# A sandwich layer on eight cores: the next block's K projection ahead of the receptance matmuls, or all projections at the block's start

## What is computed

```python
x = x + layernorm(attn(layernorm(x)))   # q,k,v projections, rope, 16 heads of 64,
                                        # band: a query sees itself and the 512 keys before it; wo
x = x + layernorm(ffn(layernorm(x)))

# ffn, per token, x_prev = the token before:
xr = mu_r * x + (1 - mu_r) * x_prev
xk = mu_k * x + (1 - mu_k) * x_prev
r = sigmoid(xr @ W_r.T)
k_act = square(relu(xk @ W_k.T))
out = r * (k_act @ W_v.T)
```

## Time and profile before

| | us |
|---|---|
| median of 2 runs | 6092.82 (6066.61 to 6119.03) |
| the profiled execution | 6056.06 |
| its span on the slowest core (5) | 6054.5 |
| spans of the eight cores | 6033.4 to 6054.5 |
| blocks | 16 |

### The profile page before, as it was taken

One profiled execution on the slowest core, in us unless ns is written; L12 is line 12 of the kernel. 1 busy time (PEld: TensorE's weight loads), 2 busy tenths in 40 slices (PEclk: granted clock), 3 DMA queues, 4 the chain that ended last, 5 costly groups with the idle time before them and its releaser, 6 DMA issues.

```text
span 6054.5 us, 52395 instructions; the slowest of 8 cores (6033.4 to 6054.5 us)
## 1 busy us (share of the span) xinstructions
PE 3191.1 (53%) x11840; PEld 1236.7 (20%) x11840; DVE 2472.7 (41%) x3561; ACT 2120.2 (35%) x3905; POOL 1200.6 (20%) x1028
## 2 busy tenths in 40 slices
PE   0344726557362664737646373673636457364573
PEld 0111212222120221212222121221212122121221
DVE  2353443434344343443435344343443534334342
ACT  0141523415233251533524244161432415244152
POOL 0021212212121121211211122121221212122122
PEclk9957567575675857658576665856658575675757
DMA  6512122120322202122121311303112130311301
GB/s 187 154 42 73 39 80 73 42 84 28 84 70 69 84 29 73 53 70 84 34 74 50 93 56 55 99 8 90 56 59 94 42 91 21 84 70 42 111 1 63
DMA packets 269844, 410.36 MB, mean 68 GB/s; under 512 B 151778, under 2 KB 151778, under 8 KB 269540
## 3 DMA queue, kind: packets, MB, share of 16 engines
q1 hardware_dynamic: 203492, 197.28, 12.3%
q0 software_dynamic: 33792, 134.22, 6.9%
q10 hardware_dynamic: 32256, 75.51, 3.2%
HBM read 297.89 MB, written 75.50 MB: 62 GB/s over the span
## 4 chain that ended last, share of the span: by engine, by line
PE 30%; ACT 20%; DVE 19%; DMA 8%; issue 8%; POOL 7%; SPq 5%; ACTq 2%; DVEq 1%; POOLq 0%
PE pb L521 7%; ACT pk L495 6%; SPq L174 4%; PE pb L488 4%; PE pb L326 4%; DVE ybuf L533 4%; PE pb L678 4%; PE pb L408 3%; PE pb L580 3%; ACT krot L250 3%; ACT krot L253 3%; DVE ax L637 3%; POOL ybuf L755 2%; POOL pk L713 2%; POOL pk L506 2%
## 5 line engine op out<-in xcount | busy, mean ns | idle before, releaser
L533 DVE RECIPROCAL ybuf<-pb 1x512 bf16<-1x512 f32 x256 | 858.0, 3352 | 805.8 <-PE pb L521 797.3
L326 PE MATMUL pb<-vext,Wwk 128*128 128x512 bf16 x1024 | 260.4, 416 | 1666.3 <-DMA vext<-hstage 1624.2
L495 ACT ACTIVATE pk<-pb,neg 128x512 bf16<-128x512 f32 (+3 forms) x1792 | 945.3, 527 | 282.7 <-PE pb L488 26.2
L488 PE MATMUL pb<-qx,krot 64*128 64x512 bf16 (+3 forms) x1792 | 681.0, 434 | 395.1 <-ACT pk L495 308.6
L521 PE MATMUL pb<-pk,vext 128*65 128x128 bf16 (+3 forms) x2368 | 522.9, 404 | 79.2 <-DVE ax L546 33.0
L326 PEld LDWEIGHTS pb<-vext,Wwk 128*128 128x128 bf16 x1024 | 104.4, 105 | 1818.8 <-issue 1727.6
L510 POOL TENSOR_TENSOR pk<-pk,tri4s 128x512 bf16<-128x512 bf16 x256 | 294.2, 1149 | 751.7 <-ACT pk L495 751.7
L506 POOL TENSOR_TENSOR pk<-pk,tri0s 128x512 bf16<-128x512 bf16 x192 | 220.8, 1150 | 1043.8 <-ACT pk L495 1043.8
L326 PE MATMUL pb<-vext,Wwq 128*128 128x512 bf16 x1024 | 256.3, 411 | 248.9 <-DVE scr L350 248.9
L730 PE MATMUL pb<-WS,pk 128*128 128x512 bf16 x1024 | 284.0, 443 | 159.2 <-DVE pk L741 71.4
L488 PEld LDWEIGHTS pb<-qx,krot 64*128 64x128 bf16 x1792 | 165.8, 107 | 965.3 <-issue 965.3
(11 more groups left out here) (105 smaller groups left out, 4046.4 us busy)
## 6 DMA issues: line engine op xcount, KB each, us to landing
xsl<-x SPq DMA_DIRECT2D x128, 512.0 KB, 4.1
WS<-wo_bf POOLq DMA_DIRECT2D x16, 2048.0 KB, 12.4
WS<-wr_bf POOLq DMA_DIRECT2D x16, 2048.0 KB, 21.1
cosb<-cosd SPq DMA_DIRECT2D x128, 256.0 KB, 4.4
sinb<-sind SPq DMA_DIRECT2D x128, 256.0 KB, 4.8
WS<-wk_bf POOLq DMA_DIRECT2D x16, 2048.0 KB, 10.4
WS<-wv_bf POOLq DMA_DIRECT2D x16, 2048.0 KB, 10.1
out<-ybuf ACTq DMA_DIRECT2D x64, 512.0 KB, 2.7
```

Source lines behind the costliest of these rows:

```text
L326: ins = e.matmul(pb[bk][:, :], wsb[:, D * ci + 128 * dc:D * ci + 128 * (dc + 1)], hv[:, BS * ci:BS * (ci + 1)], start=(ci == 0), stop=(ci ...
L488: qlo=qlo, qhi=qhi: e.matmul(pb[bk][:, qlo:qhi], ksrc[po:po + 64, BS * md + 128 * tc:BS * md + 128 * (tc + 1)], qx[po:po + 64, BS * md + q ...
L495: texp = cop("scalar", lambda e, bk=bk, c=c, qlo=qlo, qhi=qhi, pku=pku: e.activation(out=pku[:, BS * c + qlo:BS * c + qhi], in_=pb[bk][:, ...
L533: t_rc = cop("vector", lambda e, rb=recipb[uslot], ub=ub: e.reciprocal(rb, pb[ub][64:65, :]), waits=[t_av, buf.get(("recip", uslot)), prev ...
```

## The change

The blocks are no longer interleaved in that way.

- `planB1` and `planB2` are gone. At the start of each block stand all projections: Q pair 0 (banks 0, 1), K pair 0 (4, 5), Q pair 1 (2, 3), K pair 1 (6, 7), and again with p = 2 and 3; each is followed in DVE's list by its rotation. Cos and sin of a p are loaded once and serve q and k.
- v goes through banks 0 and 1 in turn; each evacuation waits only for its own group and the memset, which stands at the block's start.
- The next block's `planA` stands behind the receptance matmuls and sigmoids and before the keys. It reads the transposed layernorm output into hfm, not into vext.
- Keys use banks 4 and 5, wv2 banks 6 and 7 (both had 2 and 3).
- The square of the relu moves from GpSimd to DVE.
- The scratch tile of the statistics is now always the older vext tile. The debug output, off in both, is removed. Some tokens that guard buffers are other ones.

```diff
-        t_hr = [dmat("sync", "hfm", hv[:, BS * c:BS * (c + 1)], hstage[:, 128 * c:128 * (c + 1)],
-                     waits=[t_hw[-1], av_tok]) for c in range(8)]
+        t_hr = [dmat("sync", "hfm", hfm[:, BS * c:BS * (c + 1)], hstage[:, 128 * c:128 * (c + 1)],
+                     waits=[t_hw[-1], buf.get("hfm")]) for c in range(8)]
...
+        lnsink[0] = vext[1 - par][:, 0:2048].bitcast(F32)
+        onesap = bass.AP(vext[par][:, :].tensor, 64, [[4160, 128], [65, 64]])
+        ones_restore = cop("vector", lambda e, a=onesap: e.memset(a, 1.0),
+                           waits=[kv_cons[par]], tok=True)
...
+        load_cos(0, n)
+        load_cos(1, n)
         for p in range(4):
-            mm = _proj_mms(W["wk"], t_wres["wk"], p, (4, 5) if p % 2 == 0 else (6, 7),
-                           hv, t_hr, extra=[sinkA_tok] if p == 0 else ())
+            q_toks += proj_pair(W["wq"], t_wres["wq"], qx, buf.get("qx"), bqs, p,
+                                (0, 1) if p % 2 == 0 else (2, 3))
+            k_toks += proj_pair(W["wk"], t_wres["wk"], krot[par], kv_cons[par], bks, p,
+                                (4, 5) if p % 2 == 0 else (6, 7))
             if p + 2 <= 3:
-                load_cos(p + 2)
+                load_cos(p + 2, n)
...
-                bk = tj * 2 + hh
+                bk = (tj * 2 + hh) % 2
...
+                tev = cop("scalar", lambda e, oap=oap, bk=bk: e.copy(oap, pb[bk][:, :]),
+                          waits=[tmm, ones_restore], tok=True)
...
-        if it + 1 < niter:
-            pendingA = planA(it + 1, t_av_last)
-
-        if it + 1 < niter:
-            pendingB = planB1(it + 1, pendingA, buf.get("lnstat"))
 
         wr_users = []
         t_rsg = []
...
+        if it + 1 < niter:
+            pendingA = planA(it + 1)
+
         t_wv2 = stream_weight("wv2", 1, wr_users)
...
-            bk = 2 + dk % 2
+            bk = 4 + dk % 2
...
-            tka = cop("gpsimd", lambda e, dk=dk: e.tensor_mul(
+            tka = cop("vector", lambda e, dk=dk: e.tensor_mul(
                 pk2[0][:, BS * dk:BS * (dk + 1)], relu_t[:, :], relu_t[:, :]),
...
-                bk = 2 + hh
+                bk = 6 + hh
```

More of the change, by code:

```diff
@@ L276, in build_core @@
     prev_z = None
+    kv_cons = [None, None]
     kv_tok = [{}, {}]
@@ new lines, in planA @@
+        return t_ln, t_hw, [t_hr[-1]] * 8
+    pendingA = None
+    ones_restore = None
+    for it in range(niter):
+        s, n = it // NB, it % NB
+        par = n % 2
+        rows0 = s * S + n * BS
+        lnsink[0] = vext[1 - par][:, 0:2048].bitcast(F32)
+        onesap = bass.AP(vext[par][:, :].tensor, 64, [[4160, 128], [65, 64]])
+        ones_restore = cop("vector", lambda e, a=onesap: e.memset(a, 1.0),
+                           waits=[kv_cons[par]], tok=True)
+        if it == 0:
+            t_wo = stream_weight("wo", 0, [])
+            t_wr = stream_weight("wr", 1, [])
+            t_ln, t_hw, t_hr = planA(0)
+        else:
+            t_wo, t_wr = next_wo, next_wr
+            t_ln, t_hw, t_hr = pendingA
@@ L309, in _mk_cos, with load_cos @@
         t_cos = {}
[L311 removed]
+        def load_cos(p, n):
             slp = p % 2
[L313 removed]
+            tc1 = dma("sync", "cos%d" % slp, cosb[slp][:, :], cos_d[p, :, n * BS:(n + 1) * BS],
                       waits=[buf.get(("cos", slp))])
[L315 removed]
+            tc2 = dma("sync", "sin%d" % slp, sinb[slp][:, :], sin_d[p, :, n * BS:(n + 1) * BS],
@@ L316, in load_cos @@
                       waits=[buf.get(("cos", slp))])
             t_cos[p] = (tc1, tc2)
[L318 to L350, removed]
-            scr[:, BS:2 * BS], pb[bhi][:, :], bias_sb[:, p + 4:p + 5], cosb[slp][:, :],
-            ALU.add, ALU.mult), tok=True)
-        t6 = cop("vector", lambda e: e.tensor_add(
-            dst[:, BS * (p + 4):BS * (p + 5)], scr[:, 0:BS], scr[:, BS:2 * BS]), tok=True)
-        bank_free[blo] = t5
-        bank_free[bhi] = t5
-        buf["scr"] = t6
-        buf[("cos", slp)] = t6
-        return [t3, t6]
@@ L561, in build_core @@
                 plan_norm(head_order[i - 2])
-        t_dbg = None
-        if dbg and it == 0:
-            t_dbg = dma("sync", "z", dattn[:, :], ax[:, :], waits=t_attn_evac)
+        kv_cons[0] = kv_cons[1] = t_av_last
         wo_users = []
@@ L618, in build_core @@
         t_h2r = [dmat("sync", "hfm", hfm[:, BS * c:BS * (c + 1)], h2stage[:, 128 * c:128 * (c + 1)],
-                      waits=[t_h2w[-1], buf.get("hfm")]) for c in range(8)]
+                      waits=[t_h2w[-1]] + q_toks + k_toks + v_toks + t_sc_all) for c in range(8)]
         t_h2r = [t_h2r[-1]] * 8
```

155 lines of the change are left out of this document (64 added, 91 removed).

## The result

| | before | after |
|---|---|---|
| median, us (lowest to highest) | 6079.07 (6054.11 to 6127.35, 10 runs) | 5725.11 (5718.11 to 5784.43, 11 runs) |
| profiled execution, us | 6056.06 | 5732.47 |
| its slowest core: span | 6054.5 (core 5) | 5730.8 (core 6) |
| mean granted clock of that core, share of 2.4 GHz | 0.686 | 0.700 |

The ratio is 0.9415, with a 95% interval of 0.9377 to 0.9453: 5.9% faster. The forecast was 5622, a gain of 467 us on the profiled execution; the gain there is 324. (The before median that the forecast started from, 6092.8, was of two runs; ten give 6079.) The direction and the mechanism came out, but 143 us of the gain are missing. Where no core is named, a mean is of the profiled core: 5 in before, 6 in after.

A forecast was written before the change was run, and what follows sets the result against it. No engine is full, so a chain of waits bounds the kernel. Terms sum to 137.4 us against 167.4 per transition, 30.0 less, fifteen times; with first and last block 5589 profiled, 5622 as median; range 5506 to 5780.

The forecast's parts named there:

- (d): Output stage: from the start of the wv2 matmuls to the first product, 2.5 us.
- (a): Behind the mix: receptance matmuls follow at once, 20.9 us from mix end to the last sigmoid's end.
- (b): Behind the sigmoids: next block's layernorm on ScalarE ahead of the relus, 21.1 us, with 2 for slower x loads.
- (c): Key stage: six remaining key groups after a cold start, with relu and the square on DVE, 15.7 us.
- (e): First product to first rotation: final layernorm chain without its table load, 34.2 less 1.3, so 32.9 us.
- (f): Projections: eight rotations in a row on DVE, V after the fifth begins, 44.2 us to the last V evacuation.
- sign (2): Key groups: TensorE idle of 15 to 20 us, ended by a relu, with the next block's statistics on ScalarE.
- Sign (3): Final layernorms: no table load in them.
- The clock stays low: Rival: clock stays at 1.2 GHz from the mix on, 51 us more per transition, about 6410; chance 0.03.
- The attention keeps the full clock: Rival: ScalarE's waits for AV matmuls vanish in the attention, 248 us less, about 5370; chance 0.05.
- Traffic: Rival: x loads, transposes and cos/sin loads meet weight streams in all blocks, gain 15 per transition, about 5850; chance 0.09.
- Nothing gained: Rival: removed idle comes back whole as ScalarE's stop and DVE's rotations, about 6090; chance 0.03.

The follow-up runs named there:

- experiment 1: Changed kernel with the landing of the stores put last in the wait list of the h2stage transposing reads: 5631.54 us, ratio 0.9265.
- experiment 2: Kernel before with only the changed kernel's long wait list put behind the landing in the h2stage transposing reads: 6224.22 us, ratio 1.0237.
- experiment 6: Changed kernel with the square of the relu back on GpSimd: 5757.14 us, ratio 0.9485.
- experiment 4: Changed kernel with the next block's layernorm straight after the mix, ahead of the receptance matmuls and sigmoids: 5602.07 us, ratio 0.9243.
- experiment 7: Changed kernel with the next block's layernorm interleaved slab by slab with the mix, its stores and transposes after it: 5544.51 us, ratio 0.9128.
- experiment 8: Changed kernel with layernorm in the mix, landing last in the wait list and wo stream ahead of wv2, together: 5398.39 us, ratio 0.8892.
- experiment 3: Changed kernel with the wo stream issued ahead of the wv2 stage instead of behind it: 5712.67 us, ratio 0.9417.

## Why the prediction came out as it did

**The step that failed: "The diff leaves the attention and everything up to the end of the mix in place (only the scratch destination of the statistics and the names in some waits change)."** I took a longer wait list for free because every name in it is satisfied long before. Satisfied waits still go through the queue one by one, and these stand behind the one that comes last, so their 50 ns apiece all lie on the path: 16 blocks lose 6.5 us, 104 of the 143 that are missing. Experiments 1 and 2 show it in both kernels. The prediction said for the moved transposes of hstage that "SP's queue holds nothing else that is due", and was right; the same question was not asked of h2stage. The range held, but by a cost that none of its terms stood for, and with luck: the 5732 of the profiled execution lie above the 5718 that all its worst terms together gave, and only what was added on top (0.6%, and the widening to 5780) takes them in.

The rest by steps, means over the 15 transitions, in us:

| step | forecast | measured | |
|---|---|---|---|
| before, whole interval | 167.4 | 167.7 | a fair average in total, not in each step: see (d) |
| (a) receptance | 21.0 | 22.6 | second pair cold in 8 of 15 |
| (b) layernorm on ScalarE | 21.1 | 21.0 | |
| (c), (d) to the first product | 18.2 | 17.0 | (d) is 1.8, not 2.5; the square takes 0.43, not 0.75 |
| (e) to the first rotation | 32.9 | 33.7 | the second product comes later |
| (f) to the last V evacuation | 44.2 | 45.7 | cos/sin stall, cold V |
| sum | 137.4 | 140.0 | |

(a) The receptance matmuls do follow the mix at once, at 2545.42 in block 6 with the mix's end at 2545.60. Block 6 takes 21.5. The mean is higher since the second pair of groups runs cold in 8 of the 15 transitions. TensorE in block 6, then in block 7:

```profile
2545.42 5.70 PE L626 MATMUL pb<-WS,qx 128*128 128x512 bf16 x16 [70.36 <-DVE qx L596]
2553.24 3.61 PE L626 MATMUL pb<-WS,qx 128*128 128x512 bf16 x15 [2.12 <-ACT qx L637]
```

```profile
2899.14 6.32 PE L626 MATMUL pb<-WS,qx 128*128 128x512 bf16 x16 [69.28 <-DVE qx L596]
2907.58 5.30 PE L626 MATMUL pb<-WS,qx 128*128 128x512 bf16 x15 [2.12 <-ACT qx L637]
```

The pause between them is the same 2.12 us (it ends with ScalarE's sigmoids); the clock survives it in one block and not in the other. These 8 blocks take 23.6 to 24.1, the other 7 20.7 to 21.5. The range had this as "a second cold receptance pair", at 1.8; the measured step between the two kinds is some 2.7, and about half of that belonged into the sum.

(b) As forecast, and mostly for its own reasons: of the traffic allowance of 2, some 1.5 is there. ScalarE's third slab waits 3.1 us for x in the mean, where before waited 1.6, and the step varies with it from 19.2 to 23.0. In block 6 it waits 2.67, where before waited 1.46; the last row is the first relu:

```profile
2578.44 1.06 ACT L249 ACTIVATE vext<-xsl 128x1024 f32<-128x1024 f32 x1 [2.67 <-DMA xsl<-x]
...
2587.65 0.60 ACT L661 ACTIVATE urt<-pb 128x512 bf16<-128x512 f32 x1 [2.00 <-DVE htm L296]
```

It follows the stores and DVE's last normalization, and the key matmuls' idle of 19.18 ends with it: sign (2), 15 to 20 us.

(c), (d) The square and the first product in block 6, and the final layernorm's reciprocal:

```profile
2588.35 0.43 DVE L664 TENSOR_TENSOR pk<-urt 128x512 bf16<-128x512 bf16 x1 [1.51 <-ACT urt L661]
...
2605.10 0.69 DVE L690 TENSOR_TENSOR aof<-pb,qx 128x512 f32<-128x512 f32 x1 [2.14 <-PE pb L679]
...
2611.24 0.16 DVE L262 RECIPROCAL rst<-sdt 128x1 f32<-128x1 f32 x1 [0.40 <-ACT sdt L260]
```

The square was mis-sized: 0.75 was the duration of an operation of another kind (L633). The Trainium skill (VectorE: DVE Perf Modes, the perf-mode tier table) gave an estimated 0.42, and the trace agrees with it. For the path this is 0.3. The larger part of what (c) and (d) came out shorter is in (d). From the first value matmul to the first product is 1.78 us in every block of after, where the forecast took 2.5 from block 6 of before. That block was one of the quick ones: the mean of before is 3.6, since its value matmuls mostly restarted cold (experiment 6). So the change also took a cold start out of most blocks, which the forecast did not have in its sum for either kernel.

(e) No table load: DVE waits 0.40 for the root of the first tile, as it did for the later ones in before. Sign (3) holds. Block 6 takes 33.5, against 34.2 less 1.3: the first product comes earlier than in before, but the second follows 1.73 later, where before had 1.18 in this block (2775.79 and 2776.97 in its trace), so a part of what (d) gained is given back here. The 1.28 of the load itself is saved in full: where the table load is back in this stage, in experiments 4, 7 and 8, the step is 35.0 in the mean, 1.3 more than the 33.7. The dearer table switch that the Trainium skill states (ScalarE: Activation LUTs, What ACT_TABLE_LOAD costs), by which 1.4 more would have been saved, did not show.

(f) The rotations go at 5.14 to 5.29 us, eight in a row. In block 6 the fifth is 2.1 us late for its sine (experiment 3), and TensorE's V begins 4.26 after it, as forecast, but after a pause of 3.79 and cold:

```profile
2666.22 3.31 PE L391 MATMUL pb<-Wwv,hfm 128*128 128x512 bf16 x8 [3.79 <-DVE scr L361]
...
2684.52 0.39 PE L395 MATMUL pb<-bvr,onesb 1*128 1x512 bf16 x1
```

18.7 instead of 17.3. V's evacuations are spread under it: the last ends 0.7 us after the last matmul (2684.99 + 0.59). The cos/sin stall was given as 0.5 and is 1.6 in the mean on this core (6.90 between the fourth and the fifth rotation less 5.3; 1.0 to 1.6 over the eight), and goes when the wo stream is moved (experiment 3). It was inside its bound of 5. The cold start of V that comes with it in 8 of the 15 transitions was in no term.

Outside the sum: the first block gave 19.4 for the 16 forecast, the last 6.1 for the 1. Of the latter I had counted the square alone; before had a cold value stage there (10.01 us for its first 32 matmuls, where hot ones take 7.07), and after has none.

The books: waits on SP 104, reads that took longer 13, 15 transitions at 2.3 less than forecast 35, together 152, less 8.5 from the first and last block: 143.5 for the 143 missing. The forecast's 0.6% between the profiled execution and the median went the other way in the new kernel (5725 median, 5732 profiled), which took 40 off, so that 5725 stands against 5622.

**The rivals.** *The clock stays low*: refuted, 0.90 to 0.96 from the first product on. *The attention keeps the full clock*: refuted, 0.52 in the part of the attention shown, with TensorE busy 77% of it, and its length 116.5 against 116.7. *Traffic*, at 5850: real but small, 1.8 us a transition by experiment 3 and 1.5 at x in (b); the measured time lies between its 5850 and the 5622 for another reason. *Nothing gained*: refuted; the relu's idle (19.7 for the forecast's 17) and the rotations came about as sized. (Its sum, 30 + 15 + 5 less 17 and 21, leaves 12, not the 30 of the forecast: not all that was saved stands in it.) None of the rivals had the wait list in it.

What stays open: why the same pause costs the clock in one block and not in the next, and how much of experiment 4 is the x loads.

## What to carry to other kernels

Compare the wait lists of the steps that a change leaves "in place", and count the waits by instruction, not by whether they are satisfied: put the one that comes last at the end of the list, and where many counts of one semaphore stand in it, keep the highest (the order was tried here, the merging not). When several engines take turns, look for the engine that is idle in the neighbouring stage before moving work to a faster one: the layernorm in the mix gave 2.9%, while the square on DVE gave under 1%, which the times alone do not resolve, most of it by shortening a pause of TensorE. Price such a pause by what like pauses in the trace did to the granted clock: here 1.6 us was free, and 2.1 to 2.7 cost a restart in 8 of 15, 13 of 15 and 6 of 15 cases. Look at more than one block for it: the block that the forecast read was one of the 4 of 16 whose value matmuls had started hot.

## What the runs showed of the hardware

- A satisfied wait on SP's queue takes about 50 ns, of which 17 are the record of the instruction: 143 waits take 7.49 us, 79 of them 4.34.
- The same pause of 2.12 us, between the same matmuls, cost the granted clock in 8 of 15 blocks and left it in 7; the pause of 3.79 ahead of V in block 6 cost it (two of 2.9 and 3.1 in other blocks did not, 8 matmuls in 1.89 us), and one of 1.64 ahead of the value matmuls did not in any of the 16 blocks (31 matmuls in 6.85 us, the hot rate of the earlier trace rows). The 3.04 of before cost it in most of 16. With the square on GpSimd that pause is 2.65, and cost it in 13 of 15 transitions on one core and in 6 of 15 on another.
- DVE's bf16 product of 512 columns, all in SBUF, takes 0.43 us, GpSimd's 1.04.
- A normalization from f32 to bf16 of 1024 columns takes 0.81 us on DVE, and 1.62 with a GpSimd product beside it (experiment 7).
- A table load of ScalarE takes 1.28 us, and a stage with one more of them on its path is 1.3 us longer (35.0 against 33.7).
